# A deformable convolution whose row weights are computed inside its main loop instead of in a stage of their own

## What is computed

```python
om = conv2d(x, w_off, padding=1) + b_off            # 27 channels: 9 y-offsets, 9 x-offsets, 9 logits
off_y, off_x, mask = om[:, :9], om[:, 9:18], sigmoid(om[:, 18:])
py = off_y + row + ky                                # ky, kx in -1, 0, 1 for the 9 taps
px = off_x + column + kx
sampled = bilinear(x, py, px) * mask                 # zero outside the image
out = einsum("bckhw,ock->bohw", sampled, w) + b
out = (out - mean) * rsqrt(var + 1e-5) * gamma + beta   # statistics over all images
return relu(out) + x
```

## Time and profile before

| | us |
|---|---|
| median of 3 runs (lowest, highest) | 2331.4 (2331.2, 2337.84) |
| span of the profiled execution | 2334.2 |
| first block pair, up to the first matmul of the offset convolution | 206.4 |
| offset convolution, its last store issued and landed | about 351 |
| row weights and the restart, up to the first `sample` | 352 to 700 |
| main loop, first to last `sample` | 700 to 2102 |
| exceptions, batch norm, output | 2102 to 2334 |

### The profile page before, as it was taken

The page is one execution under the profiler, slowest core; times in us unless marked ns, Lnnn a source line. Parts: engine busy times, 40 slices in busy tenths (PEclk is TensorE's granted clock), DMA queues, the critical chain, the costliest instruction groups (busy, mean ns, idle before and its releaser), DMA issues. The chain is left out here.

```text
span 2334.2 us, 61913 instructions
## 1 busy us (share of the span) xinstructions
PE 1539.5 (66%) x24206; PEld 1050.0 (45%) x24207; DVE 1558.4 (67%) x1718; ACT 1449.8 (62%) x2219; POOL 606.7 (26%) x1168
## 2 busy tenths in 40 slices
PE   4755980000008888888898898898888898891620
PEld 4632330000006666666665566666665666660310
DVE  5342006656717888888888788888887888883105
ACT  2221224344218898888898898898887898890102
POOL 2000000000033444444443444444444444430000
PEclk9688995555558999999999999999999999996555
DMA  2177874667675666666666666566666656640008
GB/s 116 32 190 184 233 218 159 215 227 275 235 214 126 151 147 157 149 149 155 150 148 152 148 149 157 149 150 157 149 146 150 152 147 157 149 100 22 3 0 338
DMA packets 288861, 362.19 MB, mean 155 GB/s; under 512 B 61853, under 2 KB 260820, under 8 KB 285014
## 3 DMA queue, kind: packets, MB, share of 16 engines
q1 hardware_dynamic: 209552, 226.57, 37.6%
q0 software_dynamic: 36864, 59.94, 11.2%
q10 hardware_dynamic: 42182, 72.05, 9.0%
HBM read 253.94 MB, written 104.39 MB: 154 GB/s over the span
## 5 line engine op out<-in xcount | busy, mean ns | idle before, releaser
L758 POOL DMA_DIRECT2D rows<-scratch_parts x1152 | 583.1, 514 | 821.1 <-PE ps_even_y L790 798.8
L799 PE MATMUL ps_odd_y<-rows,sel 32*128 32x504 f32 (+2 forms) x928 | 459.8, 496 | 502.5 <-DMA rows<-scratch_parts 345.2
L939 DVE TENSOR_TENSOR G<-odd_y,ps_odd_v 128x1008 f32<-128x1008 f32 (+2 forms) x464 | 542.0, 1168 | 182.5 <-PE ps_odd_v L816 182.4
L816 PE MATMUL ps_odd_v<-tent_x,stage 32*128 32x171 f32 (+2 forms) x5568 | 591.1, 318 | 0.0
L947 DVE TENSOR_TENSOR G<-even_v,ps_even_y 128x1008 f32<-128x1008 f32 (+2 forms) x464 | 539.3, 1162 | 23.6 <-ACT even_v L895 21.7
L816 PE MATMUL ps_even_v<-tent_x,stage 32*128 32x171 f32 (+3 forms) x5568 | 541.9, 324 | 8.5 <-DMA stage<-scratch_xt 8.3
L889 ACT COPY odd_y<-ps_odd_y 128x504 f32<-128x504 f32 (+2 forms) x928 | 526.4, 567 | 21.4 <-PE ps_odd_y L799 17.1
L895 ACT COPY even_v<-ps_even_v 128x1008 f32<-128x1008 f32 (+2 forms) x464 | 450.2, 970 | 134.6 <-PE ps_odd_v L816 126.5
L834 PE MATMUL ps_r<-G,conv_w 128*32 128x224 f32 (+1 forms) x8832 | 483.3, 346 | 13.2 <-ACT res L900 13.1
L799 PEld LDWEIGHTS ps_odd_y<-rows,sel 32*128 32x128 f32 x928 | 173.0, 186 | 689.8 <-issue 350.5
L816 PEld LDWEIGHTS ps_odd_v<-tent_x,stage 32*128 32x128 f32 x5568 | 477.8, 190 | 0.0
(11 more groups left out here) (134 smaller groups left out, 913.5 us busy)
## 6 DMA issues: line engine op xcount, KB each, us to landing
place<-scratch_px SPq DMA_DIRECT2D x960, 105.0 KB, 3.4
scratch_parts<-parts ACTq DMA_DIRECT2D x18, 3136.0 KB, 16.7
rows<-scratch_parts POOLq DMA_DIRECT2D x960, 52.5 KB, 3.4
x<-scratch_xh SPq DMA_DIRECT2D x48, 406.0 KB, 5.9
place<-scratch_px SPq DMA_DIRECT2D x192, 84.0 KB, 2.7
scratch_om<-om ACTq DMA_DIRECT2D x64, 196.0 KB, 7.1
rows<-scratch_parts POOLq DMA_DIRECT2D x192, 42.0 KB, 2.6
scratch_conv<-res SPq DMA_DIRECT2D x448, 14.0 KB, 1.8
```

The source lines that it names most:

```text
L758: pool.dma_start(bass.AP(tensor=rows[b][:].tensor, offset=32 * g * pitch + here, ap=[[2 * pitch, Y_KINDS], [GROUP * W, 3], [1, count * W]] ...
L799: nc.tensor.matmul(ps_odd_y[:, lo:hi], sel[32 * g:32 * g + 32, :], taps(rows, 32 * g, 32, p, lo, hi), start=True, stop=True).then_inc(odd_ ...
L816: m = nc.tensor.matmul(sub(ps_v[g // 2], 0, 128, i * 512 + lo + first, dims), stage[32 * g:32 * g + 32, j * IMAGE + v * C:j * IMAGE + (v + ...
L939: nc.vector.tensor_tensor(two(G, ROW, v, slot(v)), two(odd_y[p % 3], ROW, v), two(ps_v[1], 512, v), ALU.mult).then_inc(odd_weighted, 1)
```

## The change

The block of row weights is gone. The offset convolution and the main loop become one block, so their tiles live side by side: `x3`, `om` and the sigmoid lie in the end and start of `G`, which has 18 slots instead of 20. The channels of the offset convolution are reordered, its rows sorted by parity, and `om` in DRAM becomes a table by kind (`PX`, `OY`, `MASK`), parity, tap and slot, so that a load takes nine taps at once; slots that no row fills are zeroed by 18 small DMAs in the block before.

In the offset convolution each PSUM chunk is read by ACT (sigmoid of all 128 rows, line 846) and by DVE (line 924: offsets, with tap and column added); DVE then takes maximum and minimum (930) and merges sigmoid and offsets (935). The store is 24 DMAs a pair, 12 from ACT's queue and 12 from SP's.

The row weights of pair it + 2 are made during pair it. SP loads `dense_y` and `dense_m` (126 x 464) at step 3. POOL makes nine clips of y (675), each 128x464, and one subtraction of neighbours (679, 128x3712), which gives the negative tent minus the offset. DVE adds 1 and multiplies by the mask, eight instructions of 128x464 behind `cap` in steps 9 to 16 (910). SP stores them at step 18 as one DMA. High and low are no longer stored: SP loads the weights twice, for ten steps at once ("double", three `rows` buffers), and POOL splits them on chip: `high` is the rounded copy in the low half of the partitions (690) and is subtracted (696). The loads of `rows` move from POOL's queue to SP's: 48 a pair, `place` 24 instead of 72.

```diff
-            @block.scalar
-            def _(act):
...
-                def front(n):
...
-                    nc.scalar.activation(sorted_rows(mask[b]), by_parity(logit[b]), ACT.Sigmoid).then_inc(masked, 1)
-                    for r in range(WIN):
-                        a = nc.scalar.activation(sorted_rows(tent_y[b], r), by_parity(oy[b]), ACT.Abs, bias=shift[:, r:r + 1])
...
-                    nc.vector.tensor_scalar(tent_y[b][:, :], tent_y[b][:, :], 1.0, 1.0,
-                                            ALU.min, ALU.subtract).then_inc(capped, 1)
...
+            def store_om(eng, pair, half):
+
+                b = pair % 2
+                for h in range(2):
+                    for ky in range(3):
+                        for r in range(2):
+                            j = 2 * half + h
+                            eng.dma_start(dram("om", (pair * 2 + half) * OM_IMG + ((r + ky) % 2 * KK + ky * 3) * SL
...
+                for pair in range(PAIRS):
+                    b = pair % 2
+                    wait(act, om_stored[b], 16 * STORES * (pair // 2))
+                    for ch in range(NCH):
+                        act.wait_ge(convolved, pair * NCH + ch + 1)
+                        nc.scalar.activation(sub(G, 0, 128, SIG_AT[b] + ch * CH, [[1, CH]]), ps_o[ch % 2][:, 0:CH],
+                                             ACT.Sigmoid, bias=boff[:, 0:1]).then_inc(masked, 1)
+                    if pair:
+                        act.wait_ge(merged, pair)
+                        store_om(act, pair - 1, 1)
...
+                    for tile, op in zip(ranges, (ALU.max, ALU.min)):
+                        r = nc.vector.tensor_reduce(tile[:, pair * HALF_UNITS:(pair + 1) * HALF_UNITS],
...
+                    nc.vector.scalar_tensor_tensor(sig, sig, is_mask[:, 0:1], sub(G, 0, 128, OM_AT[b], [[1, OM]]),
...
+                        if p % (2 * GROUP) == 0 and double_of(it, p) + 2 < ALL_DOUBLES:
...
+                            load_rows(double + 2)
+                        if p == 3 and it + 2 < PAIRS:
+                            load_dense(it + 2)
+                        if p == 18 and it + 2 < PAIRS:
+                            store_parts(it + 2)
...
+                    for k in range(WIN + 1):
+                        at = float(k - BASE_SHIFT - 1)
+                        nc.gpsimd.tensor_scalar(tent_y[:, k * DCH:(k + 1) * DCH], dense_y[:, :], at, at + 1.0,
+                                                ALU.max, ALU.min).then_inc(clipped, 1)
...
+                    nc.gpsimd.tensor_tensor(w, w, tent_y[:, DCH:], ALU.subtract).then_inc(differed, 1)
...
+                for double in range(1, ALL_DOUBLES):
+                    split(double)
+                    if double % DOUBLES == 1 and double // DOUBLES + 2 < PAIRS:
+                        tents(double // DOUBLES + 2)
...
+                    nc.vector.scalar_tensor_tensor(w, w, 1.0, dense_m[:, :], ALU.add, ALU.mult).then_inc(weighted, 1)
...
                             cap(*to)
+                        if 9 <= p < 9 + WIN and it + 2 < PAIRS:
+                            mask_kind(it + 2, p - 9)
```

587 lines of the change are left out of this document (299 added, 288 removed).

## The result

The changed kernel takes 2992.2 us (median of 4 runs, 2991.1 to 2992.9) against 2334.6 us for the kernel before in the same session: a ratio of 1.281, 95% interval 1.277 to 1.285. The prediction was 2306 us, faster at 0.62. It is wrong in sign and outside its range. The profiled execution has a span of 2990.9 us.

A forecast was written before the change was run, and what follows sets the result against it. No engine alone bounds the kernel; a ring through PE, ACT and DVE sets the main loop's step. 2334.2 - 225.7 (up to first `sample`) + 187 (loop) + 13 (exceptions) = 2308.5, less 2.8: 2306 us; range 2120 to 2430.

The forecast's parts named there:

- Covered: Main loop: POOL's 72 issues go, SP's 151 DMAs (148 before) and DMA share 0.74 (0.63 before) stay hidden, adding no time.
- The date of the tents: Main loop: `dense_y` lands near 14 us into the pair, tents ready near 27, first mask near 29; two us in hand.
- the covered date slips: Rival, main loop: with POOL at its upper bounds the first mask waits 3 us a pair, +40; no separate chance given.
- POOL's rates: Main loop: one-input instructions 1.0 ns a column (clip 0.5 us), two-input 2.2 ns (subtraction 8.2 us); 37 us a pair.
- Does POOL hold up DVE?: Main loop: two-column or two-input DVE instructions wait for the POOL instruction in progress; 13.0 us a pair, +187 in all; chance 0.40.
- The third case: Rival, main loop: POOL gets its turn between `cap` and mask; 21.4 us a pair, +305, total 2424; chance 0.20.
- The convolution: Offset convolution: chain from sigmoid through stores back to PE, 15.5 us a pair, 248 us for 16, masks +5.
- the whitening: Block before the convolution: 18 small DMAs ahead of the first store in SP's queue, +8 us, bounds 0 to 20.
- the restart: Between the convolution's end and the first `sample`: some 7 us, with `place`, `stage` and first weights already loaded.
- The exceptions: Range and unit loads: ranges in 4096 pieces +11, the unit's loads +4, smaller reductions -2; +13 us in all.
- The 18 slots: Main loop: 216 extra matmul pieces of 60 ns each, covered by PE's 0.3 to 0.4 us a step.

The follow-up runs named there:

- the version whose transfers are in time: Changed kernel with `rows` loads spread at pitch 4, dense loads made one DMA per image and issued at step 19 of the pair before: 2406.7 us, ratio 1.034.

## Why the prediction was wrong

**"Covered" is the step that failed.** It counted DMAs (151 against 148 a pair), and MB as a share of 0.74, and priced neither the shape of a DMA nor what stands behind it in one queue. The loads of `rows` went from 16 partitions spread over a group, on POOL's queue, to eight neighbours on SP's; their rate had no term. They ran at 70 GB/s, and `place`, the dense loads and the stores of `res`, all behind them in SP's queue, kept ACT waiting up to 19 us and POOL longer. "If that cover fails, PE waits for `rows` or `stage`" named the risk without a price and with the wrong victims: ACT waited for `place` and for room in `res`, POOL for `dense_m`. These are 239 + 168 us of waits; with the tents' 204, the longer `cap`s' 54 and masks' 74, and their own 18, that makes 757, beside the 776 us that the loop grew. That the sum comes so near is in part luck: waits need not add up, and the run with POOL's arithmetic cut gave back less than its share of them. Spreading the partitions and splitting and moving the dense loads took back 0.247 of the ratio.

**The date of the tents, "two us in hand".** The dense loads were to land near 14 us into the pair and the tents to be ready 13 later. They took 24 us (9 clips of 1.78 and the subtraction of 8.0), and `dense_m` landed some 24 us after its issue. The first mask waited 14.6 us in each of 14 pairs. The rival "the covered date slips" had the mechanism at +40; it was 204 us of waits.

**POOL's rates.** The two-input estimate was good: 8.0 us for the subtraction (8.2 forecast) and 2.13 for a third of a double (1.85, and that includes waiting for DVE). The one-input estimate, scaled from a memset, was low by a factor of more than 3: clips take 3.8 ns a column, over twice the upper bound of two passes (1.7). The prediction named this as a way to be wrong, and it was.

**Does POOL hold up DVE?** Yes, in the way assumed: a `cap` that meets a POOL instruction waits for the whole of it, 8.17 us beside 8.04. Size: forecast 169 us without the masks' own 18, measured 136 in the version whose transfers are in time. That version's loop, 1599 us, lies near the forecast 1589 partly by luck, for POOL's part is smaller than forecast and the rest (62 us) larger. In the changed kernel itself it is less visible (`cap` at most 2.13 us), since DVE stands still, waiting for the tents, while the long subtraction runs. The third case, POOL's turn between `cap` and mask, which had 305 us, was not tested by itself; taking the masks away gave 53 us in all, so it is not where the time goes.

**The convolution.** Right chain, short links. Forecast 15.5 us a pair, within 13.8 to 17.8, and 5 in all for masks; measured 20.9, these masks included. The issue was taken at 0.47 us, from stores of 32 partitions; of three by three rows it takes 0.75. The landing was taken as 2.2 us from a store of 14 KB; it took 3.4 to 9.7, with a median of 5.0. The first is a duration carried over from a DMA of another shape. What makes the landing long stays open: with the next input's load behind the stores it still took 1.4 to 20 us. First `sample` 572.6 instead of 474.4: 3.6 of it in the whitening (11.6 instead of 8), 82 in the convolution with the masks between its pairs, 13 in the restart (20 instead of 7).

**Smaller terms.** The exceptions and what follows cost +8.5 where +13 was forecast. The 18 slots brought 432 more matmuls of `reduce` (9264 after 8832), not 216.

Why the sign was wrong: the forecast spent all its chance on what DVE and POOL do to each other and on DMA volume, and none on the rate of a DMA changing with its shape. With the loads spread, split and issued in time, and nothing else changed, the kernel stands at 1.034 instead of the forecast 0.988; most of what is left between these, 107 us, is the convolution, 329 us where 253 were forecast, and the restart behind it, 20 instead of 7.

## What to carry to other kernels

When a change alters which partitions a DMA fills, or the outermost size of its access pattern, price it anew: look for a stretch of the trace where only that kind runs and read GB/s and share together, since the share tells runs apart that have the same rate (here 0.42 and 1.11 at 121 and 122 GB/s), and a low rate at a share like 0.56 says that the engines are busy and get little done. Before moving a transfer to another queue, list what will stand behind it there and who waits for each of these. Where GpSimd computes beside VectorE, try keeping the hot VectorE instruction out of the two-columns form even if it is longer alone (0.42 to 0.67 us here bought 95 us of loop), and keep GpSimd's instructions short.

## What the runs showed of the hardware

- The same 16 DMAs of 8 partitions run at 70 GB/s on neighbours and at 121 GB/s at pitch 4; 8 DMAs of 16 neighbours run at 122 GB/s with all engines busy.
- An issue of a store of nine partitions takes SP or ACT 0.75 us when its DRAM side is three by three rows and 0.38 us when it is nine at one pitch, with the same pieces.
- A fp32 clip of 464 columns takes GpSimd 1.75 us at best, 3.8 ns a column, where a subtraction of two inputs takes 2.16 ns a column (8.0 us for 3712).
- A VectorE instruction of 504 columns on one SBUF tile, two columns at a time, took 7.7 us longer beside a GpSimd instruction of 8.04. The same work with nine rows 58 columns apart took 0.67 us, and never over 0.68, in 432 instructions.
- Writing the input as nine rows that lie end to end left `cap` at 416 ns, as one run; only a real gap between the rows changed it.
